# A cross-attention kernel in full-precision halves: softmax ahead of the former batch's probabilities, and a batch's memory in one load

## The chip, the cores and the metric

The kernel runs on 1 core of a Trainium2 chip. The metric is device time in microseconds of one execution. All inputs are in HBM, and the output is written there. Host work that only lays out the inputs is not in the time.

## The reference

Per batch (32 of them), x is 112 x 512 and the memory 375 x 256. In float32:

```
memory_proj = memory @ W_mem.T                      # 375 x 512
scores      = x @ memory_proj.T / sqrt(512)         # 112 x 375
attn        = softmax(scores)
context     = attn @ memory_proj                    # 112 x 512
gate        = sigmoid(concat([x, context]) @ W_gate.T + b_gate)
fused       = x + gate * context
out         = fused * rsqrt(mean(fused**2) + 1e-6) * norm_w
```

## The kernel before

**Reassociation.** The projected memory is never formed. q = x W_mem (112 x 256 per batch) meets the raw memory for the scores; `am` = attn times raw memory (112 x 256); the context is am W_mem.T; and the gate's second half is am times `wga`, a product of two weights made once in the opening.

**Halves.** A float32 product is made of three matmuls on rounded operands: high by high, low by high, high by low. Every operand X therefore exists as `X_hi` (ScalarE, `high`, line 537, a copy that rounds) and `X_lo` (the remainder: DVE `low`, line 694, or POOL `low`, line 878). `product` (lines 357 to 359) runs the high stationary operand first (lines 347 and 349) and the low one last (line 354), so that an attend can begin when `pT_hi` is ready and needs `pT_lo` only for its last third (lines 389 to 399).

**Tiling.** A group is 8 batches, 896 rows of x, 7 tiles of 128 rows; there are 4 groups. A step s handles, in each engine's own written order: the scores and softmax of batch s, the attend of batch s-1, the high and low halves of am of batch s-2, the gate and context product of one tile t = `tile_at(s)`, and the end (gate_context, fuse, square, norm) of the tile before. In steps with s % 8 == 2 there is no tile. `q_pieces_at` puts the products for q into steps with s % 8 in 0, 1, 3 (two of them), 6 and 7; `x_unit_at` the splits of xT. Step 30 handles batches 30 and 31, the second one late (`softmaxes_at`).

**Softmax of batch s.** TensorE's scores go to one PSUM bank. DVE: `maximum` (reduce, line 706, then line 708, which multiplies by -1/sqrt(512)). ScalarE: `exponentials` (line 566, scale 1/sqrt(512), bias the shift, row sum into `total`). DVE: `turn_p` (line 714) transposes 32 x 32 blocks into `blocks_p`; SP moves them in 4 DMAs of 48 KB to `pT_raw` (`move_p`, line 262), which completes the transpose; ScalarE and DVE make `pT_hi`, `pT_lo` (lines 572 and 722). `am` goes the same way: copied out of PSUM by ScalarE (line 579), turned by DVE (line 728), moved by SP in 4 DMAs (line 269), then halved.

**Orders around the change.** In step s, ScalarE: pT_high(s-1), exponentials(s), amT_high(s-2), square, split_memT(s+1), attended(s-1), split_mem(s), q_high, split_xT, tanh (lines 658 to 684). In step 30 split_memT(31) stands before the exponentials. DVE: gate_context, pT_low(s-1), maximum(s), fuse, turn_p(s), shares, amT_low(s-2), turn_am(s-1), norm, q_low, add_bias (lines 836 to 863). POOL: the inverse root for the tile before, memT_lo(s+1), mem_lo(s), xT_lo (lines 911 to 922); in step 30 memT_lo(31) first. TensorE: score(s), gate_x, attend(s-1), q pieces, gate_am, context (lines 512 to 529).

**SP's queue** is one order by hand (lines 281 to 336). In step s: move_p(s), move_am(s-1), load_memT(s+3), load_mem(s+1), an xT unit, and the x rows and the output of a tile. `memT_raw` and `mem_raw` have two slots each; `blocks_p` and `pT_raw` have one, so move_p(n) waits for pT_lo(n-1).

Of the kernel before, what the change touches and what calls it, by code (L numbers as in the profile page):

```python
# [12 lines left out]
P = 128  # L13
# [13 lines left out]
MEMT, MEM = EC * KEVEN, KC * E  # L27
UNITS = [(0, 256), (256, 320), (576, 320)]
# [74 lines left out]
def build_gated_cross_attention(nc, x_d, xT_d, memT_d, mem_d, first_d, wmT_d, wgT_d, b_d, nw_d, out_d):  # L103
    ctx = ExitStack()
    with ctx:
# [10 lines left out]
        first_raw = sb("first_raw", [P, DC // 2 * (E + UNITS[0][1])])  # L116
# [11 lines left out]
        memT_raw = sb("memT_raw", [P, 2, MEMT])  # L128
        mem_raw = sb("mem_raw", [P, 2, MEM])
# [3 lines left out]
        blocks_p = sb("blocks_p", [P, KPAD])  # L133
        pT_raw = sb("pT_raw", [P, KPAD])
        pT_hi, pT_lo = (sb(f"pT_{s}", [P, 2, KC, P], F32R) for s in ("hi", "lo"))
# [6 lines left out]
        top = sb("top", [ROWS, 2])  # L142
# [9 lines left out]
        zeros = blocks_p[:, 0:D // 2].bitcast(BF16)  # L152
# [6 lines left out]
        memT_raws = memT_raw[:].rearrange("p s (c n) -> p s c n", c=EC)  # L159
        mem_raws = mem_raw[:].rearrange("p s (c n) -> p s c n", c=KC)  # L160
        firsts = [first_raw[:], work[:, 4:6].rearrange("p s d -> p (s d)")]
        wm_halves = [a[:, 0:DC // 2 * E].rearrange("p (i e) -> p i e", e=E) for a in firsts]
        x0_halves = [a[:, DC // 2 * E:].rearrange("p (i n) -> p i n", i=DC // 2) for a in firsts]
        wmT_raw = first_raw[:].rearrange("p (c d) -> p c d", c=EC)
# [7 lines left out]
        turned_p = blocks_p[:].rearrange("p (j c r) -> p c j r", j=Q, r=R)  # L172
        pT_flat = pT_raw[:].rearrange("p (q n) -> p q n", q=Q)
        pT_rows = pT_raw[:].rearrange("p (q c r) -> p c q r", q=Q, r=R)
        blocks_p_rows = [blocks_p[R * q:R * (q + 1)].rearrange("p (j n) -> p j n", j=Q) for q in range(Q)]
# [4 lines left out]
        amT_rows = amT_raw[:].rearrange("p (q c r) -> p c q r", q=Q, r=R)  # L180

# [33 lines left out]
        memT_loaded = [sem(f"memT_loaded{i}") for i in range(2)]  # L215
        mem_loaded = [sem(f"mem_loaded{i}") for i in range(2)]
# [6 lines left out]
        scores_done, top_ready, shift_ready = sem("scores_done"), sem("top_ready"), sem("shift_ready")  # L223
        probs_ready, share_ready = sem("probs_ready"), sem("share_ready")
        blocks_p_ready, p_turned = sem("blocks_p_ready"), sem("p_turned")
# [13 lines left out]
        def _(sp):  # L239
# [7 lines left out]
            def load_memT(n):  # L247
                if n >= 2:
                    sp.wait_ge(memT_lo_ready, n - 1)
                sp.dma_start(memT_raw[:, n % 2], memT_d[n]).then_inc(memT_loaded[n % 2], 16)  # L250
# [732 lines left out]
```

## Time and profile before

| | us |
|---|---|
| three plain runs | 334.11, 334.95, 336.81 |
| their median | 334.95 |
| the profiled execution | 332.4 |
| its span | 330.2 |
| TensorE matmul busy | 285.8 (87%) |
| TensorE weight loads | 243.6 (74%) |
| DVE busy | 216.5 (66%) |
| ScalarE busy | 171.7 (52%) |
| POOL busy | 169.7 (51%) |
| DMA, mean share of 16 engines, hardware queue | 60.6% |

The span runs from the first to the last instruction of the profiled execution; its own time is 2.2 us longer. Engines are PE (TensorE matmul), PEld (its weight loads, which overlap the matmuls), DVE, ACT (ScalarE), POOL (GpSimd) and SP, whose queue issues every DMA here (SPq). All rows of instructions with the same form that follow each other are merged into one, with a count. PEclk is the granted TensorE clock as a share of 2.4 GHz.

### The profile page before, as it was taken

The page shows a single profiled execution, that of the slowest core. Times are in us where ns is not written, and L with a number is a line of the kernel's source. Part 1 is how long each engine was busy: PE and PEld are TensorE (multiplying, and loading weights), DVE is VectorE, ACT ScalarE, POOL GpSimd, SP SyncE. Part 2 cuts the span into 40 slices and gives each one's busy share as a digit, 9 for nine tenths or more (in the row PEclk, how much of TensorE's full clock was granted, in tenths as well). Part 3 has the DMA queues.
Part 4 walks back from the last instruction along what each step waited for, and adds up shares of the span by engine and source line. Part 5 has one row for each costly group of instructions (what it writes and reads, how often), then busy time and mean ns, then how long its engine had stood idle before and what let it go on. Part 6 is the DMA issues. An engine that isn't in the chain of part 4 may idle for free.

```text
span 330.2 us, 4795 instructions
## 1 busy us (share of the span) xinstructions
PE 285.8 (87%) x1479; PEld 243.6 (74%) x1479; DVE 216.5 (66%) x388; ACT 171.7 (52%) x363; POOL 169.7 (51%) x135
## 2 busy tenths in 40 slices
PE   8999699899995499999997499999998499996392
PEld 4979488778884498788886498788887398884362
DVE  4995556677676536877577626777777736786344
ACT  5865354457544537456555546546555445553412
POOL 1244248555655544665658544665758543653302
PEclk9999979999999599999999599999999699999787
DMA  7959953757766293866846383766837464652411
GB/s 285 423 152 240 284 185 85 240 187 248 212 186 191 53 276 101 263 201 177 281 136 199 110 267 111 233 207 188 277 92 232 138 199 113 201 147 52 155 48 65
DMA packets 57048, 61.40 MB, mean 186 GB/s; under 512 B 39104, under 2 KB 39360, under 8 KB 56768
## 3 DMA queue, kind: packets, MB, share of 16 engines
q1 hardware_dynamic: 57024, 61.10, 60.6%
q8 instruction: 12, 0.20, 0.2%
q14 instruction: 12, 0.10, 0.1%
HBM read 43.25 MB, written 7.34 MB: 153 GB/s over the span
## 4 chain that ended last, share of the span: by engine, by line
PE 30%; DVE 20%; SPq 13%; DMA 13%; ACT 10%; issue 7%; POOL 5%; DVEq 0%; POOLq 0%
SPq L262 7%; DMA pT_raw<-blocks_p 6%; DVE pT_lo L694 6%; DMA mem_raw<-in_mem 6%; PE gate_ps L347 5%; PE gate_ps L349 4%; PE gate_ps L354 4%; SPq L269 4%; POOL memT_lo L878 3%; DVE work L743 3%; ACT work L593 2%; DVE top L706 2%; DVE work L737 2%; PE score_ps L347 2%; ACT probs L566 2%
## 5 line engine op out<-in xcount | busy, mean ns | idle before, releaser
L878 POOL TENSOR_TENSOR mem_lo<-mem_raw,mem_hi 128x768 fp32r<-128x768 f32 x32 | 68.1, 2129 | 23.4 <-ACT mem_hi L537 23.4
L878 POOL TENSOR_TENSOR memT_lo<-memT_raw,memT_hi 128x752 fp32r<-128x752 f32 x31 | 56.6, 1825 | 30.0 <-ACT memT_hi L537 30.0
L896 POOL TENSOR_TENSOR guarded<-meansq,eps 128x1 f32<-128x1 f32 x27 | 5.1, 190 | 98.7 <-ACT work L588 98.7
L566 ACT ACTIVATE probs<-score_ps,shift 112x375 f32<-112x375 f32 x32 | 18.3, 573 | 56.8 <-DVE shift L708 56.8
L728 DVE STREAM_TRANSPOSE blocks_am<-am 128x256 f32<-128x256 f32 x32 | 14.3, 446 | 42.0 <-ACT am L579 38.8
L694 DVE TENSOR_TENSOR pT_lo<-pT_raw,pT_hi 128x384 fp32r<-128x384 f32 x32 | 33.0, 1031 | 11.6 <-ACT pT_hi L537 11.6
L758 DVE SCALAR_TENSOR_TENSOR work<-work,rstd,norm_w 128x512 f32<-128x512 f32 (+1 forms) x29 | 39.8, 1375 | 1.1 <-POOL rstd L931 1.0
L593 ACT ACTIVATE work<-work 128x512 f32<-128x512 f32 (+1 forms) x29 | 17.8, 616 | 36.3 <-DVE work L737 36.3
L743 DVE SCALAR_TENSOR_TENSOR work<-work,ctx_ps 128x512 f32<-128x512 f32 (+1 forms) x28 | 19.0, 679 | 23.9 <-ACT work L593 22.0
L537 ACT ACTIVATE mem_hi<-mem_raw 128x768 fp32r<-128x768 f32 x32 | 26.9, 840 | 13.7 <-DMA mem_raw<-in_mem 13.7
L347 PE MATMUL gate_ps<-wgx_hi,xT_hi 128*128 128x512 f32 x108 | 32.0, 422 | 0.1
L347 PE MATMUL score_ps<-memT_hi,qT_hi 128*112 128x376 f32 x64 | 18.2, 368 | 15.3 <-POOL memT_lo L878 14.8
L349 PE MATMUL gate_ps<-wgx_lo,xT_hi 128*128 128x512 f32 x108 | 29.8, 399 | 0.0
L354 PE MATMUL gate_ps<-wgx_hi,xT_lo 128*128 128x512 f32 x108 | 28.9, 389 | 0.0
L537 ACT ACTIVATE memT_hi<-memT_raw 128x752 fp32r<-128x752 f32 x32 | 26.2, 820 | 0.0
L347 PEld LDWEIGHTS score_ps<-memT_hi,qT_hi 128*112 128x112 f32 x64 | 11.1, 189 | 20.2 <-issue 17.3
L347 PE MATMUL am_bank<-mem_hi,pT_hi 128*112 128x256 f32 x96 | 17.4, 290 | 9.9 <-POOL mem_lo L878 6.3
L347 PEld LDWEIGHTS am_bank<-mem_hi,pT_hi 128*112 128x112 f32 x96 | 14.6, 178 | 14.6 <-issue 7.1
L537 ACT ACTIVATE pT_hi<-pT_raw 128x384 fp32r<-128x384 f32 x32 | 16.4, 514 | 16.5 <-DMA pT_raw<-blocks_p 16.5
L878 POOL TENSOR_TENSOR xT_lo<-xT_raw,xT_hi 128x1280 fp32r<-128x1280 f32 (+1 forms) x9 | 24.8, 2761 | 0.0
L349 PEld LDWEIGHTS gate_ps<-wgx_lo,xT_hi 128*128 128x128 f32 x108 | 20.9, 194 | 4.9
L347 PEld LDWEIGHTS gate_ps<-wgx_hi,xT_hi 128*128 128x128 f32 x108 | 21.8, 209 | 3.6 <-DVE work L737 0.8
(125 smaller groups left out, 665.0 us busy)
## 6 DMA issues: line engine op xcount, KB each, us to landing
mem_raw<-in_mem SPq DMA_DIRECT2D x32, 384.0 KB, 4.1
memT_raw<-in_memT SPq DMA_DIRECT2D x32, 376.0 KB, 3.5
x_rows<-in_x SPq DMA_DIRECT2D x28, 256.0 KB, 4.5
out<-work SPq DMA_DIRECT2D x27, 256.0 KB, 4.7
pT_raw<-blocks_p SPq DMA_DIRECT2D x128, 48.0 KB, 2.5
xT_raw<-in_xT SPq DMA_DIRECT2D x7, 640.0 KB, 6.3
amT_raw<-blocks_am SPq DMA_DIRECT2D x128, 32.0 KB, 1.9
xT_raw<-in_xT SPq DMA_DIRECT2D x3, 512.0 KB, 5.8
```

What stands on the lines that cost most here:

```text
L262: sp.dma_start(pT_flat[:, q], blocks_p_rows[q]).then_inc(p_turned, 16)
L347: pe.matmul(out, l_hi, r_hi, start=first and i == 0, stop=False)
L349: pe.matmul(out, l_hi, r_lo, start=False, stop=False)
L354: mm = pe.matmul(out, l_lo, r_hi, start=False, stop=last and i == len(lefts) - 1)
L537: return act.activation(out, in_, ACT.Copy)
L566: act.activation(probs[0:ROWS, 0:KEYS], scores[:, 0:KEYS], ACT.Exp, bias=shift[:, n % 2:n % 2 + 1], scale=D ** -0.5, accum_out=total[:, n ...
L593: act.activation(z[:, t % 2, cols], z[:, t % 2, cols], ACT.Tanh, scale=0.5).then_inc(tanh_ready, 1)
L694: return dve.tensor_tensor(out, in_, high.bitcast(F32), ALU.subtract)
L728: dve.transpose(turned_am, am_blocks).then_inc(blocks_am_ready, 1)
L743: dve.scalar_tensor_tensor(out=u[:, cols], in0=z[:, t % 2, cols], scalar=1.0, in1=bank[:, cols], op0=ALU.add, op1=ALU.mult).then_inc(u_rea ...
L758: dve.scalar_tensor_tensor(out=y[:, t % 2, cols], in0=h[:, t % 2, cols], scalar=rstd[:, t % 2:t % 2 + 1], in1=norm_w[:, cols], op0=ALU.mul ...
L878: return pool.tensor_tensor(out, in_, high.bitcast(F32), ALU.subtract)
```

## The change

- **Order.** In each step ScalarE does the exponentials of batch s before pT_high(s-1); DVE does maximum(s), fuse, turn_p(s) and shares(s) before pT_low(s-1). The opening's order on both engines stays.
- **Two buffers.** `blocks_p` and `pT_raw` get two slots and `p_turned` becomes two semaphores, so move_p(n) waits for pT_lo(n-2) only. `pT_hi` and `pT_lo` lie in `wgc_hi`, and pT_high(0) waits for the products that read it.
- **Scale.** 1/sqrt(512) is applied in q_high and q_low. The exponentials lose their scale; the maximum is one reduce with `negate=True`, and the instruction of line 708 is gone.
- **Memory.** From batch 3 on, memT and mem of a batch come in one DMA of 760 KB into one of three slots (the third is `first_raw`), issued in step s for batch s+2 after move_p(s) and move_am(s-1), and waiting for both low halves of the slot's former batch. In the opening memT(2) is issued earlier relative to move_p(0), and mems(3) and mems(4) stand after move_am(0) and move_am(1). The wmT load goes to `work` and waits for the wgc splits.

```diff
+MEMS = MEMT + MEM
+RAW = 3
...
+        blocks_p = sb("blocks_p", [P, 2, KPAD])
+        pT_raw = sb("pT_raw", [P, 2, KPAD])
...
+        raws = [mems_raw[:, 0], mems_raw[:, 1], first_raw[:]]
...
+            def load_mems(n):
+                sp.wait_ge(memT_lo_ready, n - RAW + 1)
+                sp.wait_ge(mem_lo_ready, n - RAW + 1)
+                sp.dma_start(raws[n % RAW], mems_d[n]).then_inc(mems_loaded[n % RAW], 16)
 
             def move_p(n):
                 sp.wait_ge(blocks_p_ready, n + 1)
-                if n >= 1:
-                    sp.wait_ge(pT_lo_ready, n)
+                if n >= 2:
+                    sp.wait_ge(pT_lo_ready, n - 1)
                 for q in range(Q):
-                    sp.dma_start(pT_flat[:, q], blocks_p_rows[q]).then_inc(p_turned, 16)
+                    sp.dma_start(pT_flat[n % 2][:, q], blocks_p_rows[n % 2][q]).then_inc(p_turned[n % 2], 16)
...
             load_mem(0)
-            load_memT(2)
             load_xT(0, 2)
-            move_p(0)
-            sp.wait_ge(wm_hi_ready, 2)
-            sp.wait_ge(wm_lo_ready, 2)
+            sp.wait_ge(wm_hi_ready, 1)
+            sp.wait_ge(wm_lo_ready, 1)
             sp.wait_ge(x0_hi_ready, 1)
             sp.wait_ge(x0_lo_ready, 1)
-            sp.wait_ge(xT_hi_ready, 1)
-            sp.wait_ge(xT_lo_ready, 1)
+            load_memT(2)
+            move_p(0)
             load_mem(1)
+            sp.wait_ge(wgc_lo_ready, DC)
             sp.dma_start(wmT_raw, wmT_d).then_inc(wmT_loaded, 16)
-            load_memT(3)
             move_p(1)
...
             load_mem(2)
             move_am(0)
-            load_memT(4)
+            load_mems(3)
             move_p(2)
...
             move_am(1)
-            load_memT(5)
-            load_mem(3)
+            load_mems(4)
...
-                if s + 3 < BATCHES:
-                    load_memT(s + 3)
-                if s + 1 < BATCHES:
-                    load_mem(s + 1)
+                if s + 2 < BATCHES:
+                    load_mems(s + 2)
...
-                high(qT_hi[:, half, c:c + w], banks[n % 2][:, 0:w]).then_inc(q_hi_ready, 1)
+                act.activation(qT_hi[:, half, c:c + w], banks[n % 2][:, 0:w], ACT.Copy,
+                               scale=D ** -0.5).then_inc(q_hi_ready, 1)
...
                 act.activation(probs[0:ROWS, 0:KEYS], scores[:, 0:KEYS], ACT.Exp,
-                               bias=shift[:, n % 2:n % 2 + 1], scale=D ** -0.5,
+                               bias=shift[:, n % 2:n % 2 + 1],
                                accum_out=total[:, n % 2:n % 2 + 1]).then_inc(probs_ready, 1)
...
-                if s - 1 < BATCHES:
-                    pT_high(s - 1)
                 if late:
                     split_memT(s + 1)
                 for n in softmaxes_at(s)[:1]:
                     exponentials(n)
+                if s - 1 < BATCHES:
+                    pT_high(s - 1)
...
                 dve.wait_ge(scores_done, n + 1)
-                dve.tensor_reduce(top[:, s], scores[:, 0:KEYS], AX.X, ALU.max).then_inc(top_ready, 1)
-                dve.wait_ge(top_ready, n + 1)
-                dve.tensor_scalar(shift[:, s], top[:, s], -D ** -0.5, None, ALU.mult).then_inc(shift_ready, 1)
+                dve.tensor_reduce(shift[:, s], scores[:, 0:KEYS], AX.X, ALU.max, negate=True).then_inc(shift_ready, 1)
...
-                if s - 1 < BATCHES:
-                    pT_low(s - 1)
                 for n in softmaxes_at(s)[:1]:
                     maximum(n)
                 if before is not None:
                     fuse(before)
                 for n in softmaxes_at(s)[:1]:
                     turn_p(n)
                     shares(n)
+                if s - 1 < BATCHES:
+                    pT_low(s - 1)
```

## Rows read from the trace of the kernel before

**Rows 1.** The page: busy times, and granted clock in 40 slices

```profile
PE 285.8 (87%) x1479; PEld 243.6 (74%) x1479; DVE 216.5 (66%) x388; ACT 171.7 (52%) x363; POOL 169.7 (51%) x135
PEclk9999979999999599999999599999999699999787
```

**Rows 2.** Windows, TensorE alone: window, length, busy, clock, DMA share, GB/s

```profile
113.80:176.00 62.20, 61.19 (x334) 0.99 0.68 204
188.80:251.00 62.20, 61.19 (x333) 0.99 0.67 203
```

**Rows 3.** Timeline at boundaries (steps 10, 18): start, us, engine, line, op [idle before <-releaser]

```profile
111.61 0.94 PE L347 MATMUL score_ps<-memT_hi,qT_hi 128*112 128x376 f32 x2 [4.49 <-POOL memT_lo L878]
...
178.09 2.91 POOL L878 TENSOR_TENSOR xT_lo<-xT_raw,xT_hi 128x1280 fp32r<-128x1280 f32 x1
178.34 0.69 DVE L743 SCALAR_TENSOR_TENSOR work<-work,ctx_ps 128x512 f32<-128x512 f32 x1 [0.70 <-ACT work L593]
178.94 2.48 DVE L694 TENSOR_TENSOR pT_lo<-pT_raw,pT_hi 128x384 fp32r<-128x384 f32 x1
181.34 0.54 DVE L706 TENSOR_REDUCE top<-score_ps 112x1 f32<-112x375 f32 x1
181.48 0.60 PE L354 MATMUL am_bank<-mem_hi,pT_lo 128*112 128x256 f32 x3 [1.75 <-DVE pT_lo L694]
182.97 0.62 ACT L588 ACTIVATE work<-work 128x512 f32<-128x512 f32 x1
186.57 0.94 PE L347 MATMUL score_ps<-memT_hi,qT_hi 128*112 128x376 f32 x2 [4.49 <-POOL memT_lo L878]
```

**Rows 4.** Timeline of an ordinary step, 17

```profile
170.29 0.55 DVE L694 TENSOR_TENSOR pT_lo<-pT_raw,pT_hi 128x384 fp32r<-128x384 f32 x1
...
172.00 0.51 PE L347 MATMUL am_bank<-mem_hi,pT_hi 128*112 128x256 f32 x3
...
172.69 0.50 PE L354 MATMUL am_bank<-mem_hi,pT_lo 128*112 128x256 f32 x3
...
173.00 0.82 ACT L537 ACTIVATE memT_hi<-memT_raw 128x752 fp32r<-128x752 f32 x1
...
174.22 0.45 DVE L728 STREAM_TRANSPOSE blocks_am<-am 128x256 f32<-128x256 f32 x1 [1.05 <-ACT am L579]
```

**Rows 5.** Timeline of step 20, from turn_am to the load

```profile
204.78 0.45 DVE L728 STREAM_TRANSPOSE blocks_am<-am 128x256 f32<-128x256 f32 x1 [1.80 <-ACT am L579]
...
207.78 0.59 SPq L250 DMA_DIRECT2D memT_raw<-in_memT  x1
```

**Rows 6.** Landing: mem's issues on the page (last: median us), one in the chain

```profile
mem_raw<-in_mem SPq DMA_DIRECT2D x32, 384.0 KB, 4.1
...
170.22 5.10 DMA mem_raw<-in_mem
```

**Rows 7.** Timeline of the end, steps 30 to 32

```profile
290.62 0.82 ACT L537 ACTIVATE memT_hi<-memT_raw 128x752 fp32r<-128x752 f32 x1
290.69 0.59 SPq L255 DMA_DIRECT2D mem_raw<-in_mem  x1
...
292.18 0.57 ACT L566 ACTIVATE probs<-score_ps,shift 112x375 f32<-112x375 f32 x1 [0.74 <-DVE shift L708]
...
300.70 0.61 PE L347 MATMUL am_bank<-mem_hi,pT_hi 128*112 128x256 f32 x3 [2.53 <-ACT pT_hi L537]
...
304.03 0.59 SPq L255 DMA_DIRECT2D mem_raw<-in_mem  x1
...
310.97 0.95 PE L347 MATMUL am_bank<-mem_hi,pT_hi 128*112 128x256 f32 x3 [6.10 <-POOL mem_lo L878]
```

**Rows 8.** Windows after that: busy of PE, PEld, DVE, ACT, POOL; clock, DMA share

```profile
311.00:316.00 5.00, 5.00 (x17) 4.32 (x18) 2.15 (x5) 1.20 (x3) 0.74 (x2) 0.50 0.03 7
```

**Rows 9.** Timeline of the opening

```profile
29.32 0.82 ACT L537 ACTIVATE memT_hi<-memT_raw 128x752 fp32r<-128x752 f32 x1
...
32.83 0.51 PE L347 MATMUL score_ps<-memT_hi,qT_hi 128*112 128x376 f32 x2
...
41.58 0.71 PE L347 MATMUL gate_ps<-wga_hi,amT_hi 128*128 128x512 f32 x2 [3.34 <-ACT amT_hi L537]
```

More of the change, by code:

```diff
@@ L180, in build_gated_cross_attention @@
         amT_rows = amT_raw[:].rearrange("p (q c r) -> p c q r", q=Q, r=R)
+        pT_hi, pT_lo = (wgc_hi[:].rearrange("p c d -> p (c d)")[:, i * 2 * KPAD:(i + 1) * 2 * KPAD].rearrange(
+            "p (s c n) -> p s c n", s=2, c=KC) for i in range(2))
         def pT_slot(a, n):
@@ L547, in split_memT @@
             def split_memT(n):
-                act.wait_ge(memT_loaded[n % 2], 16 * (n // 2 + 1))
-                high(memT_hi[:, n % 2], memT_raws[:, n % 2]).then_inc(memT_hi_ready, 1)
+                if n < RAW:
+                    act.wait_ge(memT_loaded[n], 16)
+                else:
+                    act.wait_ge(mems_loaded[n % RAW], 16 * (n // RAW + 1))
+                high(memT_hi[:, n % 2], memT_raws[n % RAW]).then_inc(memT_hi_ready, 1)
             def split_mem(n):
-                act.wait_ge(mem_loaded[n % 2], 16 * (n // 2 + 1))
-                high(mem_hi[:, n % 2], mem_raws[:, n % 2]).then_inc(mem_hi_ready, 1)
+                act.wait_ge(mems_loaded[n % RAW], 16 * (n // RAW + 1))
+                high(mem_hi[:, n % 2], mem_raws[n % RAW]).then_inc(mem_hi_ready, 1)
             def q_high(g, unit, half, banks=q_ps):
@@ L721, in pT_low @@
                 dve.wait_ge(pT_hi_ready, n + 1)
-                low(pT_slot(pT_lo, n), pT_rows, pT_slot(pT_hi, n)).then_inc(pT_lo_ready, 1)
+                low(pT_slot(pT_lo, n), pT_rows[n % 2], pT_slot(pT_hi, n)).then_inc(pT_lo_ready, 1)
             def turn_am(n):
@@ L800, in _ @@
             dve.wait_ge(memT_hi_ready, 1)
-            low(memT_lo[:, 0], memT_raws[:, 0], memT_hi[:, 0]).then_inc(memT_lo_ready, 1)
+            low(memT_lo[:, 0], memT_raws[0], memT_hi[:, 0]).then_inc(memT_lo_ready, 1)
             q_low(0, 1, 0)
@@ L886, in split_memT @@
                 pool.wait_ge(memT_hi_ready, n + 1)
-                low(memT_lo[:, n % 2], memT_raws[:, n % 2], memT_hi[:, n % 2]).then_inc(memT_lo_ready, 1)
+                low(memT_lo[:, n % 2], memT_raws[n % RAW], memT_hi[:, n % 2]).then_inc(memT_lo_ready, 1)
             def split_mem(n):
                 pool.wait_ge(mem_hi_ready, n + 1)
-                low(mem_lo[:, n % 2], mem_raws[:, n % 2], mem_hi[:, n % 2]).then_inc(mem_lo_ready, 1)
+                low(mem_lo[:, n % 2], mem_raws[n % RAW], mem_hi[:, n % 2]).then_inc(mem_lo_ready, 1)
             def inverse_rms(t):
@@ L967 @@
         "xT": xT,
-        "memT": chunked(memT).reshape(BATCHES, P, MEMT),
-        "mem": chunked(turned_rows(padded(memory, 1, KPAD))).reshape(BATCHES, P, MEM),
+        "mems": np.concatenate([chunked(memT).reshape(BATCHES, P, MEMT),
+                                chunked(turned_rows(padded(memory, 1, KPAD))).reshape(BATCHES, P, MEM)], axis=2),
         "first": np.concatenate([chunked(w_memT.T).reshape(P, 2, DC // 2 * E),
```

67 lines of the change are left out of this document (32 added, 35 removed).

## The prediction, made before the changed kernel ran

> **What bounds the kernel now.** I read the page first. TensorE is busy 87% of the span, no other engine over 66%, and the granted clock falls five times [rows 1]. So the question is where TensorE isn't busy. Cut by window, it is busy 61.19 us of 62.20 in the long stretch between two group boundaries, and as much in the next one [rows 2]. A microsecond saved elsewhere is worth nothing there, and a microsecond that TensorE has to wait is lost whole. Its idle time lies in three places: the opening (3.34 us ahead of the gate's product at 41.58 [rows 9]); the group boundary, three times (1.75 and 4.49 us [rows 3]); and the last two batches (2.53 and 6.10 us [rows 7]). After the last of these the granted clock is 0.50 of full, 1.2 GHz, for 5.00 us in which TensorE is busy throughout [rows 8]: that costs another 2.5.
>
> The boundary (steps 10, 18, 26) is a step with no tile, so TensorE has only 2 us of its own work and the softmax chain is exposed. In step 18, `pT_lo` of batch 17 takes 2.48 us where the same operation takes 0.55 in an ordinary step, since POOL's `xT_lo` runs from 178.09 to 181.00; the maximum starts only at 181.34, then exponentials, fuse, square (182.97), POOL's inverse root and its `memT_lo`, and the scores of batch 19 start at 186.57 [rows 3].
>
> The profiled execution took 332.4 us for a span of 330.2; the three plain runs have a median of 334.95, 2.55 above it. I work out a difference against the profiled one and put it on the median. A measurement can tell about 1% here (3.3 us).
>
> **Maximum and exponentials first, at the boundary.** gate_context (one input in PSUM) took 0.69 us in spite of POOL's split [rows 3], so the maximum, which reads PSUM, should not be held either: it starts when gate_context ends, at 179.1, 2.2 us earlier; without L708 the exponentials start 0.55 later, at 179.7. Next on DVE is the fuse. It reads two SBUF operands, as `pT_lo` does, so it takes over the collision: POOL is done at 181.0, and pT_lo ended 0.4 after that; I put the fuse's end at 181.5. The square then starts at 181.55 instead of 182.97, and square to scores stays 3.60: 185.15. That is -1.4 a boundary, three times -4.2. Bounds: -3 (a fuse that isn't held) and +0.5 (`pT_hi` of batch 17, now done before the exponentials, comes behind them, at 180.5, and its attend starts at 181.05, some 2.3 later than now; if that lets the clock fall one step longer, the gain is gone). I take the middle, nearest to the pT_lo row.
> The Trainium skill (SBUF — State Buffer, section SBUF: two separate sides) says that a DVE operation with two SBUF inputs and a GpSimd operation take a shared port in turn, each for its whole instruction. By that rule too the fuse ends at about 181.0 plus its own 0.7, 181.7, and the boundary gives 1.2 instead of 1.4. The trace agrees with it (2.48 against 0.55).
>
> **The same order in the covered stretches.** Step 17 [rows 4]: pT_lo ends at 170.84, and the attend wants pT_hi at 172.00 and pT_lo at 172.69. After: maximum at 170.3, where pT_lo stood (TensorE's scores are there by then), 0.54 long, exponentials at 171.0, done with their accumulator read at 171.75, pT_hi 171.8 to 172.3: 0.3 late. Turned probabilities from 171.7, 0.58; reciprocal 0.12; pT_lo 0.55: ends at 173.0, wanted (0.3 later by now) at 173.0. So 0.3 us in such a step. Against it: the exponentials come 0.75 sooner (0.55 of pT_lo, 0.2 for L708 and its wait), pT_high (0.51) now stands between them and the copy of am, so that copy and what follows it on DVE come 0.25 sooner, and part of the loss is made good. In the step behind the other xT split the fuse is held as at the boundary and pT_lo comes behind it: up to 1.2 late, once a group. Together, between -0.5 and +3 a group.
>
> **The memory's loads.** This is where I see the cost. Before, memT of a batch is issued 3 steps ahead, mem one step. After, both come in one transfer issued in step s for batch s+2, behind the moves of that step, and the first half is wanted in step s+1, ahead of the copy of am on ScalarE. That closes a ring which was not there: turn_am, four SP issues (2.5), load, landing, memT_hi, am, turn_am. From rows: turn_am at 204.78 to the load's issue at 207.78 is 3.00 [rows 5]; mem, issued some 0.6 behind memT (its issue lasts 0.59), lands 4.1 after its issue (median [rows 6]), so both are there 4.7 after the first issue, and the joined transfer, which moves the same bytes with one issue less, is put at the same 4.7; from the start of memT_hi (173.00) to that of turn_am (174.22) it is 1.22 [rows 4], with the handover ahead 1.3. Sum 9.0 to 9.1 us a step. Before, eight steps took 75.0 (the scores at 111.61 to those at 186.57 [rows 3]). One of them has two pieces of q and takes TensorE 11.1 of its own work; 11.1 + 7 x 9.1 = 74.8. So the ring sits just at the mean of the steps: it costs nothing where TensorE needs more, and steps of 7.6 to 8.5 (no q piece) can no longer run ahead. Bounds: 0, and, with the landing of 5.10 that the chain shows at 170.22, 5.7 with the issue ahead [rows 6], 7 x 1.0 = +7 a group. I take +1.2 a group for ring and late halves together, three groups: +3.6.
> The Trainium skill speaks both ways here (DMA: Bandwidth & Descriptors, section Rules for kernel authors): larger transfers reach more bandwidth, and a load should be issued early and waited for late. In this trace the second counts: memT is issued up to three steps ahead now, one after. By the first, the joined load would land before 4.7; no row here shows it.
>
> **The opening.** memT of batch 3 was loaded early and split at 29.32; after, it comes with mem behind move_am(0), where memT(4) is issued now, at about 29.6; by 4.7 it lands at 34.3. ScalarE holds attended(1), amT_high(0), mem_high(2) behind it, TensorE's scores of batch 3 start at 37.1 instead of 32.83 [rows 9]: 1.8 for the two splits' handover and POOL's half are in it. The stall of 3.34 at 41.58 takes most of that back: it waits for amT of batch 1, whose move is held by the queue of x loads. Net +1 at 45, and with the ring binding in the next five steps TensorE is about 2.5 late at step 10. The boundary's idle time takes that up except for 0.5. Value +0.5, bounds 0 and +3. The alias of pT_hi on wgc_hi waits for matmuls that end before the probabilities land: nothing. q's scale in q_high and q_low is in instructions that are there already: nothing, and nothing plausible on either side.
>
> **The end.** Before, mem(31) is issued at 304.03, since SP stood at move_p(31), and the two splits and attend(31) at 310.97 follow [rows 7]. After, it comes with memT(31), issued in step 29 near 291.2 (the load of that step was issued at 290.69), and 4.4 later, with little else in the queue, it is there: 295.6. But in step 30 ScalarE splits memT(31) first (290.62) and then does the exponentials (292.18 [rows 7]): they now start at 296.5, 4.3 late. Counting on by durations of the same operations: pT_hi(29) 297.3, attend(29) 297.8, where TensorE went from step 29 to it without a pause before; attend 1.03, scores 1.2, gate 1.4, bias 0.7, tanh 0.65, pT_hi 0.5: attend(30) at 303.4 (was 300.70); am's move lands 304.9, amT_hi, square, am, mem_hi to 307.4, mem_lo 1.85: attend(31) at 309.4. So the 6.10 and 2.53 of idle mostly turn into idle before attend(29), gain -1.5. What goes with it is the slow clock: TensorE waits little before attend(31), so 5.00 us at 0.50 become 2.5 at 1.00: -2.5. Together -4.0; bounds -11 (the load isn't late) and 0 (fallen clock in steps 30 and 31 instead).
>
> **Sum.** -4.2 + 3.6 + 0.5 - 4.0 = -4.1: 328.3 profiled, and 330.9 on the median, say 331.0.
>
> **The rivals.**
> 1. Slower by the ring, 340. Landings as at 170.22 in half of the steps: 3.4 a group in place of 1.2, +6.6, one more late load in the opening (+1), one at the end (+1): -4.1 + 8.6 = +4.5, and with rounding 340. It decides from a mean landing of about 5.2 (ring 9.6, +3.5 a group). For it: such a landing stands in the trace; x, xT and output transfers share the queue. Against: the median is 4.1, and one issue goes away. Chance 0.22.
> 2. The loads are hidden, 320. Ring 0, exponentials of batch 30 on time, and both waits of the end gone: -4.2 + 0.5 - 8.6 - 2.5 = -14.8. For it: three slots, and the slot is free in time. Against: the load stands behind two moves on SP. Chance 0.14.
> 3. Late probabilities, 336. pT_hi and pT_lo cost 0.3 in some 20 steps without being made good (+6), less the 1 counted: +1. For it: TensorE is 98% busy in the stretches. Against: DVE's round shortens. Chance 0.14.
> 4. The new order does nothing at the boundary (fuse as late as pT_lo was, clock slow longer), 335: -4.1 + 4.2. Chance 0.12.
> The forecast, 327.5 to 334.5: 0.38.
>
> **The numbers.** Faster by over 1% (under 331.6): rival 2 and somewhat more than half of the forecast's band and its neighbours, 0.41. Within 1%: the rest of the band, rivals 3 and 4, 0.36. Slower: rival 1, 0.23. The range runs from 323 to 341; the likeliest case has 327.5 to 334.5.
>
> **What would show it.** Right: in steps 10, 18, 26 the maximum starts within 0.2 us of gate_context's end and the fuse takes over 1.5 us; scores of the next step 1 to 2 us sooner; memT_hi shows waits for the joined load in many steps; TensorE idle about 4 us before attend(29), under 1.5 before attend(31), no slow clock behind it; turn_am to turn_am near 9.1 in steps without q. Wrong: memT_hi never waits for a load (rival 2), or landings over 5.2 and steps of 9.6 and more (rival 1), or attends waiting for pT in most steps (rival 3).

## The result, and the profile after

The changed kernel takes 344.50 us (median of four runs, 341.96 to 344.70) against 335.11 for the kernel before on the same chip: a ratio of 1.0257, 95% interval 1.0194 to 1.0321. The forecast was 331.0 with a range to 341, so the sign was wrong and the time lies above the range. The profiled execution took 344.57 us, its span is 342.8. The spans of the two profiled executions differ by 12.6 us; the times by 9.4 on the medians. Two runs of the experiments below lie far outside the others (408.21 us in two_loads, 1005.77 us in opening) and are left out, so medians and ratios are of the undisturbed runs.

The page of the kernel after, busy times and granted clock in 40 slices, to be read against [rows 1]:

```profile
PE 295.7 (86%) x1479; PEld 246.7 (72%) x1479; DVE 210.1 (61%) x356; ACT 173.7 (51%) x363; POOL 173.3 (51%) x135
PEclk9999699999999599999999589999999689998997
```

No engine took over: DVE, ScalarE and POOL have no larger share than before. The same page, groups of instructions (busy us, mean ns, then the idle time ahead of them and what ended most of it) and DMA issues (KB each, median us to landing):

```profile
L736 DVE STREAM_TRANSPOSE blocks_am<-am 128x256 f32<-128x256 f32 x32 | 14.2, 445 | 70.5 <-ACT am L588 70.5
...
L540 ACT ACTIVATE memT_hi<-mems_raw 128x752 fp32r<-128x752 f32 x22 | 18.3, 831 | 34.6 <-DMA mems_raw<-in_mems 34.5
...
mems_raw<-in_mems SPq DMA_DIRECT2D x20, 760.0 KB, 5.1
...
first_raw<-in_mems SPq DMA_DIRECT2D x9, 760.0 KB, 4.8
```

The second line is the new thing. ScalarE's `memT_hi` stood idle for the joined load, 34.5 us in all for the two slots of `mems_raw` (and 9.0 more for the third, `first_raw`); DVE's turn_am, which stands behind it through the copy of am, waited 70.5 us.

The timeline of an ordinary step without a stall in TensorE's own row shows the ring whole, that is, the chain that leads from one turn_am over the load back to the next turn_am:

```profile
221.79 0.45 DVE L736 STREAM_TRANSPOSE blocks_am<-am 128x256 f32<-128x256 f32 x1 [1.46 <-ACT am L588]
222.26 2.48 SPq L277 DMA_DIRECT2D amT_raw<-blocks_am  x4
...
224.84 0.54 SPq L263 DMA_DIRECT2D first_raw<-in_mems  x1
...
230.05 0.84 ACT L540 ACTIVATE memT_hi<-first_raw 128x752 fp32r<-128x752 f32 x1 [1.75 <-DMA first_raw<-in_mems]
...
230.96 1.82 POOL L886 TENSOR_TENSOR memT_lo<-first_raw,memT_hi 128x752 fp32r<-128x752 f32 x1 [1.76 <-ACT memT_hi L540]
...
231.28 0.45 DVE L736 STREAM_TRANSPOSE blocks_am<-am 128x256 f32<-128x256 f32 x1 [2.86 <-ACT am L588]
...
233.04 0.57 PE L350 MATMUL score_ps<-memT_hi,qT_hi 128*112 128x376 f32 x2
```

From turn_am to the load's issue 3.05 us, from the issue to memT_hi 5.21, from memT_hi to the next turn_am 1.23: 9.49. The next turn_am starts at 240.78, again 9.50 later. TensorE is tied in by POOL: memT_lo ends at 232.78, the scores start at 233.04. The starts of three other turn_am give the mean:

```profile
134.54 0.45 DVE L736 STREAM_TRANSPOSE blocks_am<-am 128x256 f32<-128x256 f32 x1 [1.65 <-ACT am L588]
...
201.75 0.45 DVE L736 STREAM_TRANSPOSE blocks_am<-am 128x256 f32<-128x256 f32 x1 [3.37 <-ACT am L588]
...
212.89 0.45 DVE L736 STREAM_TRANSPOSE blocks_am<-am 128x256 f32<-128x256 f32 x1 [1.65 <-ACT am L588]
```

The first two lie seven steps apart, 67.2 us: 9.6 a step. The eighth is the step with two pieces of q and takes 11.14, as it did before (11.12). Together they are 78.35, the length of a group.

What that does to TensorE stands in windows of TensorE alone (window, length, busy, clock, DMA share, GB/s). Each runs from the scores behind one boundary to the scores at the next (batches 11 to 18), the first before the change, the second after, and holds the same 346 records of matmuls:

```profile
111.61:177.59 65.98, 64.97 (x346) 0.98 0.66 196
```

```profile
115.29:185.14 69.85, 67.94 (x346) 0.96 0.64 185
```

The same work takes 3.9 us longer, and in the next group (batches 19 to 26) again 3.9 (69.98 for 66.05). Only 0.9 of it shows as idle; busy rose from 65.0 to 67.9, and the busy share alone would have hidden the loss. Part of that busy time is a slower clock. The first 6 us behind the second boundary, before and after:

```profile
186.57:192.57 6.00, 6.00 (x25) 0.73 0.62 170
```

```profile
193.46:199.46 6.00, 6.00 (x16) 0.53 0.65 183
```

TensorE is busy throughout in both, but after the change it gets half the clock (1.2 GHz) for nearly all of it. Behind the other two boundaries it is 0.56 for 0.75 and 0.51 for 0.71. That is 1.2 us a group (an estimate: 6 us times the difference). The rest of the rise wasn't traced row by row.

The boundary, step 18, timeline, to be read against [rows 3]:

```profile
186.22 2.90 POOL L886 TENSOR_TENSOR xT_lo<-xT_raw,xT_hi 128x1280 fp32r<-128x1280 f32 x1
186.24 0.69 DVE L751 SCALAR_TENSOR_TENSOR work<-work,ctx_ps 128x512 f32<-128x512 f32 x1 [0.70 <-ACT work L602]
...
186.84 0.54 DVE L716 TENSOR_REDUCE shift<-score_ps 112x1 f32<-112x375 f32 x1
187.30 2.36 DVE L758 SCALAR_TENSOR_TENSOR work<-work,x_rows 128x512 f32<-128x512 f32 x1
...
188.55 0.71 PE L350 MATMUL am_bank<-mem_hi,wgc_hi 128*112 128x256 f32 x3 [2.22 <-ACT wgc_hi L540]
...
189.70 0.63 ACT L597 ACTIVATE work<-work 128x512 f32<-128x512 f32 x1 [0.90 <-DVE work L758]
...
193.46 0.94 PE L350 MATMUL score_ps<-memT_hi,qT_hi 128*112 128x376 f32 x2 [1.77 <-POOL memT_lo L886]
```

The maximum starts as gate_context ends (186.84 and 186.93, the two overlap slightly), the fuse takes over the collision with POOL and ends 0.54 us after POOL's xT_lo, and the attend waits for pT_hi (written to `wgc_hi` now). All of that is as forecast. From gate_context to the next scores it is 7.22 us, against 8.23 in [rows 3].

The opening, timeline, against [rows 9]:

```profile
29.76 0.53 SPq L263 DMA_DIRECT2D mems_raw<-in_mems  x1
...
35.01 0.83 ACT L540 ACTIVATE memT_hi<-mems_raw 128x752 fp32r<-128x752 f32 x1 [6.10 <-DMA mems_raw<-in_mems]
...
37.98 0.94 PE L350 MATMUL score_ps<-memT_hi,qT_hi 128*112 128x376 f32 x2 [5.09 <-ACT qT_hi L566]
```

And the end, timeline of steps 30 and 31, against [rows 7]; the window below it (busy of PE, PEld, DVE, ACT, POOL; clock, DMA share, GB/s) against [rows 8]:

```profile
303.82 0.54 SPq L263 DMA_DIRECT2D mems_raw<-in_mems  x1
...
308.78 0.83 ACT L540 ACTIVATE memT_hi<-mems_raw 128x752 fp32r<-128x752 f32 x1 [4.73 <-DMA mems_raw<-in_mems]
309.51 0.56 ACT L573 ACTIVATE probs<-score_ps,shift 112x375 f32<-112x375 f32 x1
...
310.62 0.60 PE L350 MATMUL am_bank<-mem_hi,wgc_hi 128*112 128x256 f32 x3 [4.12 <-ACT wgc_hi L540]
```

```profile
312.00:317.00 5.00, 5.00 (x19) 4.50 (x20) 2.76 (x7) 1.87 (x4) 0.71 (x2) 0.68 0.28 59
```

The load of the last batch (issued at 303.82, memT_hi at 308.78) holds the exponentials of batch 30 and through them attend(29), and the clock still falls behind that wait (0.68 over these 5 us).

A ledger by where the scores of batches 3, 11, 19 and 27 start, read from the timelines of the profiled executions (us; the last column is from batch 27's scores to the span's end). The lower rows are experiments, told below:

| kernel | to batch 3 | 3 to 11 | 11 to 19 | 19 to 27 | rest |
|---|---|---|---|---|---|
| before | 32.8 | 78.8 | 75.0 | 74.9 | 68.8 |
| after | 38.0 | 77.3 | 78.2 | 78.3 | 71.1 |
| order_alone | 33.3 | 75.6 | 73.2 | 72.5 | 66.9 |
| loads_first | 38.1 | 71.0 | 72.6 | 72.3 | 63.7 |
| two_loads | 36.5 | 70.7 | 73.3 | 74.0 | 65.1 |
| loads_mid | 38.0 | 71.7 | 74.9 | 74.5 | 64.3 |
| boundary | 33.5 | 70.7 | 71.3 | 70.8 | 62.3 |

Against before, the changed kernel loses 5.2 in the opening, wins 1.5 of it back by batch 11, loses 3.2 and 3.4 in the two middle groups and 2.3 at the end: 12.6.

### The profile page after: what moved, and what is told of

The parts are those of the page before. It is cut to its first block and busy times, and to the rows that moved or that the text cites. A ratio compares the mean times of both kernels' runs of the same rounds, so it can differ in the third digit from the quotient of the medians.

```text
span 342.8 us, 4761 instructions
## 1 busy us (share of the span) xinstructions
PE 295.7 (86%) x1479; PEld 246.7 (72%) x1479; DVE 210.1 (61%) x356; ACT 173.7 (51%) x363; POOL 173.3 (51%) x135
## 5 line engine op out<-in xcount | busy, mean ns | idle before, releaser
L886 POOL TENSOR_TENSOR memT_lo<-mems_raw,memT_hi 128x752 fp32r<-128x752 f32 x21 | 38.1, 1815 | 58.8 <-ACT memT_hi L540 58.8
L736 DVE STREAM_TRANSPOSE blocks_am<-am 128x256 f32<-128x256 f32 x32 | 14.2, 445 | 70.5 <-ACT am L588 70.5
L886 POOL TENSOR_TENSOR mem_lo<-mems_raw,mem_hi 128x768 fp32r<-128x768 f32 x22 | 48.1, 2188 | 10.6 <-ACT mem_hi L540 10.5
L904 POOL TENSOR_TENSOR guarded<-meansq,eps 128x1 f32<-128x1 f32 x27 | 5.5, 203 | 78.3 <-ACT work L597 78.2
L540 ACT ACTIVATE memT_hi<-mems_raw 128x752 fp32r<-128x752 f32 x22 | 18.3, 831 | 34.6 <-DMA mems_raw<-in_mems 34.5
L758 DVE SCALAR_TENSOR_TENSOR work<-work,x_rows 128x512 f32<-128x512 f32 (+1 forms) x29 | 34.4, 1189 | 0.3
L350 PE MATMUL gate_ps<-wgx_hi,xT_hi 128*128 128x512 f32 x108 | 33.2, 433 | 0.1
L352 PE MATMUL gate_ps<-wgx_lo,xT_hi 128*128 128x512 f32 x108 | 31.8, 419 | 0.0
L350 PE MATMUL am_bank<-mem_hi,wgc_hi 128*112 128x256 f32 x96 | 18.3, 300 | 12.8 <-ACT wgc_hi L540 10.8
L350 PEld LDWEIGHTS am_bank<-mem_hi,wgc_hi 128*112 128x112 f32 x96 | 14.0, 179 | 19.6 <-ACT wgc_hi L540 18.0
L357 PE MATMUL am_bank<-mem_hi,wgc_hi 128*112 128x256 f32 x96 | 19.1, 311 | 9.5 <-DVE wgc_hi L703 9.4
L352 PEld LDWEIGHTS gate_ps<-wgx_lo,xT_hi 128*128 128x128 f32 x108 | 22.3, 206 | 5.4
L886 POOL TENSOR_TENSOR memT_lo<-first_raw,memT_hi 128x752 fp32r<-128x752 f32 x10 | 18.7, 1871 | 12.5 <-ACT memT_hi L540 12.5
```

What stands on the lines that cost most here:

```text
L350: pe.matmul(out, l_hi, r_hi, start=first and i == 0, stop=False)
L352: pe.matmul(out, l_hi, r_lo, start=False, stop=False)
L357: mm = pe.matmul(out, l_lo, r_hi, start=False, stop=last and i == len(lefts) - 1)
L540: return act.activation(out, in_, ACT.Copy)
L736: dve.transpose(turned_am, am_blocks).then_inc(blocks_am_ready, 1)
L758: dve.scalar_tensor_tensor(out=h[:, t % 2, cols], in0=u[:, cols], scalar=0.5, in1=x_rows[:, t % X_SLOTS, cols], op0=ALU.mult, op1=ALU.add) ...
```

## The experiments

The kernel before was run beside each on the same chip; ratios are to it.

**loads_first.** The changed kernel with its joined load issued at the head of SP's step, ahead of both moves. The same edit of place serves as the base of later experiments.

```diff
             for s in range(OPENING, STEPS):
+                if s + 2 < BATCHES:
+                    load_mems(s + 2)
                 for n in softmaxes_at(s)[:1]:
                     move_p(n)
...
-                if s + 2 < BATCHES:
-                    load_mems(s + 2)
```

> The changed kernel, with the joined load of batch s+2 issued at the head of SP's step s, before the moves of p and am, not behind them. Theory A (a ring: turn_am, move_am, joined load, memT_hi, copy of am, 9.5 us a step): the ring is cut, memT_hi stops waiting, a group of eight steps falls from 78.2 us to 75 or less, the exponentials of batch 30 come on time; 344.5 falls to 331 to 336. The opening keeps its 3 us. Theory B (the later halves of the probabilities starve TensorE): loads don't matter, 342 to 346.

318.95 us, ratio 0.9495 (0.9449 to 0.9540). Two lines moved on one queue are worth 25.6 us, and the kernel is then 5% faster than the one before. That is 12 us below the range that the ring theory had given: it had reckoned with groups of 75 us or less, and they take 71.0 to 72.6. One step of its timeline beside the ring above:

```profile
156.89 0.38 SPq L263 DMA_DIRECT2D mems_raw<-in_mems  x1
...
159.87 2.50 SPq L270 DMA_DIRECT2D pT_raw<-blocks_p  x4
160.01 0.82 ACT L540 ACTIVATE memT_hi<-first_raw 128x752 fp32r<-128x752 f32 x1
...
162.47 2.50 SPq L277 DMA_DIRECT2D amT_raw<-blocks_am  x4
```

The load leaves 3 us ahead of the first move of its step and 8 us ahead of the place behind both moves (162.47 + 2.50) where the changed kernel has it. memT_hi doesn't wait for one here; over the whole execution it waits twice, both in the opening (5.66 and 3.30 us). The landing is longer than after the change, 6.0 and 6.2 us on the median, as the same page's DMA issues say, and costs nothing:

```profile
mems_raw<-in_mems SPq DMA_DIRECT2D x20, 760.0 KB, 6.0
...
first_raw<-in_mems SPq DMA_DIRECT2D x9, 760.0 KB, 6.2
```

Its window from the scores of batch 11 to those of batch 18 (TensorE alone, columns as above) is back at 65.8 us, for 345 records:

```profile
109.12:174.94 65.82, 65.35 (x345) 0.97 0.65 196
```

The Trainium skill (DMA: Bandwidth & Descriptors, section Rules for kernel authors) says to issue a transfer early and wait for its semaphore late. The runs agree: the longer landing that left early cost 25 us less than the shorter one that left late.

**old_order.** The changed kernel with ScalarE's and DVE's former order in each step.

```diff
+                if s - 1 < BATCHES:
+                    pT_high(s - 1)
                 if late:
                     split_memT(s + 1)
                 for n in softmaxes_at(s)[:1]:
                     exponentials(n)
-                if s - 1 < BATCHES:
-                    pT_high(s - 1)
...
+                if s - 1 < BATCHES:
+                    pT_low(s - 1)
                 for n in softmaxes_at(s)[:1]:
                     maximum(n)
...
                     shares(n)
-                if s - 1 < BATCHES:
-                    pT_low(s - 1)
```

> The changed kernel with ScalarE's and DVE's old order in the steps (pT_high before the exponentials, pT_low before the maximum); loads, two buffers and scale stay changed. Theory A: the ring doesn't pass through these, so the groups stay at 77 to 79 us and the boundary's stall comes back on top: 344 to 349. Theory B: back to 334 to 338.

352.11 us, ratio 1.0496 (1.0432 to 1.0560), 3 us above the range of the first theory: the order is worth 7.6 us even with the ring in place. It isn't the order that made the kernel slower.

**order_alone.** The kernel before with the new order and the two buffers for probabilities (`pT_hi` and `pT_lo` in `wgc_hi`, as after, to make room), and with its own loads and scales.

> The kernel before with only the new order and the two buffers for turned probabilities (pT halves in wgc_hi); separate loads in their old places, L708 and the scales as before. Theory A: the order is worth 1 to 2 us at each of three boundaries and some at the end: 327 to 333. Theory B: slower than 335.1 by 3 to 8, 338 to 343.

323.99 us, ratio 0.9629 (0.9563 to 0.9696), 12.2 us less than the kernel before beside it and 3 us below the range of the first theory. The ledger shows 1.7 to 3.2 less in each group and 1.9 less at the end. At the boundary the scores of batch 18 start at 175.09 and those of batch 19 at 182.07, 6.98 apart, where the kernel before has 177.59 and 186.57, 8.98: 2.0 less.

**two_loads.** The changed kernel with each joined load cut in two at the same place of SP's queue, memT's part first, so that memT_hi waits for 376 KB only.

```diff
-                sp.dma_start(raws[n % RAW], mems_d[n]).then_inc(mems_loaded[n % RAW], 16)
+                sp.dma_start(raws[n % RAW][:, 0:MEMT], mems_d[n, :, 0:MEMT]).then_inc(memT_loaded[n % RAW], 16)
+                sp.dma_start(raws[n % RAW][:, MEMT:MEMS], mems_d[n, :, MEMT:MEMS]).then_inc(mems_loaded[n % RAW], 16)
```

> The changed kernel with the joined load cut in two DMAs, memT then mem, issued one behind the other at the same place in SP's queue; ScalarE's split of memT waits for the first alone. Theory A: memT lands 3.3 to 3.5 us after its issue where the joined load took 5.1, the ring falls from 9.5 to 7.9 and no longer binds in most steps: groups 75 to 76, total 334 to 338, opening 1 us better. Theory B, and a theory that only the place in the queue matters and not the size: 342 to 346.

323.56 us, ratio 0.9614 (0.9551 to 0.9677), 10 us below what the ring theory had given. The page gives the landings of both parts:

```profile
mems_raw<-in_mems SPq DMA_DIRECT2D x22, 384.0 KB, 3.9
mems_raw<-in_mems SPq DMA_DIRECT2D x22, 376.0 KB, 3.5
```

memT is there 1.6 us sooner than in one transfer (3.5 against 5.1), so the ring should fall from 9.5 to about 7.9 (an estimate from these landings), and that alone gives 20.9 us. The place in the queue stayed, only the length of one link changed, so the place isn't all that matters. A shorter landing would also help a load that was merely late, without a ring, and this run can't tell the two apart. That it is a ring stands in the timeline above, where each link starts as the one before it ends and the last leads back to the first.

**am_first.** The changed kernel with `attended(s-1)` ahead of `split_memT(s+1)` on ScalarE, to take the copy of am out of the ring.

> The changed kernel with one swap on ScalarE in each step: the copy of am of batch s-1 before the split of memT of batch s+1. Loads stay where the change put them, and land 5.1 us after their issue. Theory A (it is a ring through the copy of am): the ring is cut at another place, groups fall from 78.2 to 73 to 76 us, total 322 to 330, though memT_hi still waits for its load. Theory C (the late load costs by itself, wherever ScalarE stands, since memT_lo and the scores come late): little changes, 340 to 345.

342.08 us, ratio 1.0184 (1.0108 to 1.0260). The ring theory had given 322 to 330, its rival (the late load costs by itself) 340 to 345, and the time lies with the rival. Its cause is another, though. The wait for the load did fall; what is left stands in the opening and at the end:

```profile
L540 ACT ACTIVATE memT_hi<-mems_raw 128x752 fp32r<-128x752 f32 x22 | 18.1, 824 | 12.3 <-DMA mems_raw<-in_mems 12.3
```

But memT_hi now stands behind the attend, and the timeline shows another chain:

```profile
219.57 0.62 PE L357 MATMUL am_bank<-mem_hi,wgc_hi 128*112 128x256 f32 x3 [0.47 <-DVE wgc_hi L703]
220.28 0.47 ACT L588 ACTIVATE am<-am_bank,share 112x256 f32<-112x256 f32 x1 [2.01 <-issue]
220.65 0.82 ACT L540 ACTIVATE memT_hi<-mems_raw 128x752 fp32r<-128x752 f32 x1
...
221.55 1.97 POOL L886 TENSOR_TENSOR memT_lo<-mems_raw,memT_hi 128x752 fp32r<-128x752 f32 x1 [1.29 <-ACT memT_hi L540]
...
223.78 0.57 PE L350 MATMUL score_ps<-memT_hi,qT_hi 128*112 128x376 f32 x2 [0.80 <-POOL memT_lo L886]
```

From the attend's end (220.19) the scores come 3.6 us later, where TensorE has only gate and context to do. The groups take as long as after the change (76.2, 78.3 and 78.4). In ordinary steps no load is waited for here, so its lateness can't be what they cost. One chain was cut and another made, and this run tells nothing of the size of the first.

**loads_mid.** The changed kernel with the load between move_p(s) and move_am(s-1): behind the probabilities, no longer behind am.

> The changed kernel with one edit on SP: the joined load for batch s+2 is issued after move_p(s) but ahead of move_am(s-1), so no load waits for turn_am(s-1). Theory (ring through turn_am): the ring of 9.5 us is cut, ScalarE's memT_hi no longer waits for a load in ordinary steps, groups fall from 78.2 to under 74 us, total 318 to 324. Rival (a load behind the probabilities' move is late too, because it is issued after turn_p): the load leaves 3 us sooner but still takes 5 to 6 us beside the moves, groups stay over 76, total 330 or more.

325.91 us, ratio 0.9697 (0.9645 to 0.9750): most of the gain (18.6 of 25.6), but 1.9 us above what the ring theory had given. The link from turn_am to the load is cut, and memT_hi waits for a load three times only, in the opening and at the end (11.0 us in all). The load also leaves some 3 us sooner, so a load that was merely late would have gained as well. The timeline shows what stays:

```profile
137.56 0.54 SPq L263 DMA_DIRECT2D mems_raw<-in_mems  x1
...
138.19 2.48 SPq L277 DMA_DIRECT2D amT_raw<-blocks_am  x4
...
144.88 0.42 ACT L540 ACTIVATE amT_hi<-amT_raw 128x256 fp32r<-128x256 f32 x1 [2.79 <-DMA amT_raw<-blocks_am]
...
145.82 0.82 ACT L540 ACTIVATE memT_hi<-mems_raw 128x752 fp32r<-128x752 f32 x1
```

The load for batch 15 leaves at 137.56, and memT_hi of batch 15 starts only 8.26 later. But it doesn't wait for that load: ahead of it on ScalarE stands amT_hi, which waits 2.79 for am, and the move of am is now the transfer that is issued directly behind 760 KB. Its median landing is 3.1 us here, against 1.9 in loads_first and after the change, and ScalarE waits for it 18 times, 14.2 us in all (3 times and 3.4 us in loads_first). So what is left isn't a late load, which the rival had expected, but a late move of am. That the load in front of it causes this is argued from the order of the queue and the landings; no run took it apart.

**one_buffer, scale_back.** loads_first with the waits of a single buffer for the probabilities; and loads_first with the scale in the exponentials and L708's instruction again.

> The kernel of loads_first with the waits of a single buffer of turned probabilities: move_p(n) waits for pT_lo(n-1), turn_p(n) for the move of n-1. If the second buffer is what makes the new order work (pT_lo now ends 1.2 us behind turn_p, and SP's queue stands there): 325 to 332, moves of p a good microsecond later in each step. If it only matters for batches 30 and 31: 320 to 322.

> The kernel of loads_first with the scale in the exponentials again and the maximum in two instructions. If the 0.2 us of each maximum lies on the path of every step: up to 5 us slower, 322 to 324. If it lies on the path only at the three boundaries and in the last steps: 319.5 to 320.5.

322.21 us, ratio 0.9575 (0.9496 to 0.9653), and 322.19, ratio 0.9583 (0.9510 to 0.9656): each 3.2 to 3.3 above loads_first on the medians, which were taken on another chip. one_buffer is nearer to its second case (320 to 322), scale_back lies in its first (322 to 324). The intervals overlap with that of loads_first, so each is a likely 3 us and not a proven one.

**opening.** loads_first with the opening's loads earlier: load_mems(3) after load_mem(1), load_mems(4) after move_am(0).

> The kernel of loads_first (319.0) with two loads of the opening moved forward: the joined load of batch 3 ahead of wmT and move_p(1), that of batch 4 ahead of move_p(2). Theory A2 (the opening's 4.6 us of TensorE's wait for the scores of batch 3 is that load alone): 314 to 316.5. Theory B2 (the opening's wait passes to the move of am of batch 1 behind the loads of x, 3.7 us as in order_alone): 318 to 320.

318.99 us, ratio 0.9489 (0.9390 to 0.9588): by the medians no gain, as the second theory had it. In the profiled execution the span is 314.7 against 317.7. The scores of batch 3 start at 33.15 instead of 38.09, and the gate's product then waits 3.45 us for amT at 41.78, as before the change [rows 9]. What the 5 us of the opening are worth in the end (0 to 3) stays open.

**act_back.** loads_first with ScalarE's former order alone (pT_high ahead of the exponentials); DVE keeps the new one.

> loads_first with one edit on ScalarE: pT_high(s-1) again ahead of the exponentials of batch s, as before the change; DVE keeps maximum, fuse, turn_p ahead of pT_low. It asks which half of the new order gives its 12 us. Theory A (the gain comes from exponentials that no longer stand behind a wait for the moved probabilities): the gain is lost, 328 to 332. Theory B (it comes from DVE, where the maximum no longer stands behind pT_low): at most 3 us are lost, 319 to 322.

317.13 us, ratio 0.9465 (0.9419 to 0.9511): nothing lost, 2 us below the range of the second theory. So here the order's gain doesn't need ScalarE's half; it is DVE's, where the maximum no longer stands behind pT_lo.

**boundary.** opening with another order in steps 10, 18 and 26 alone:

```diff
+                border = tile_at(s) is None and s < BATCHES - 2
-                if late:
+                if late or border:
                     split_memT(s + 1)
+                if border:
+                    pT_high(s - 1)
                 for n in softmaxes_at(s)[:1]:
                     exponentials(n)
...
```

DVE makes pT_lo between maximum and fuse in these steps, and POOL memT_lo ahead of the inverse root.

> The kernel called opening with another order in steps 10, 18 and 26 alone, where TensorE still idles 1.75 us ahead of the attend and 2.35 us ahead of the next scores: ScalarE makes memT_hi of the next batch and pT_hi of the former one while it would wait for the maximum, DVE makes pT_lo ahead of the fuse, and POOL makes memT_lo ahead of the inverse root. Theory (the two gaps are queueing behind work that can go later): 2.5 to 3.5 us less at each boundary, 8 to 10 in all, 309 to 312. Rival (what is moved behind, the exponentials and the fuse, is late next, and the gap comes back one batch on): 316 to 320.

310.42 us, ratio 0.9261 (0.9227 to 0.9295), within the theory's range and the fastest kernel of this case. The timeline of step 18:

```profile
171.83 0.51 ACT L540 ACTIVATE wgc_hi<-pT_raw 128x384 fp32r<-128x384 f32 x1
...
172.39 0.61 PE L350 MATMUL am_bank<-mem_hi,wgc_hi 128*112 128x256 f32 x3 [0.22 <-ACT wgc_hi L540]
...
173.21 2.09 POOL L892 TENSOR_TENSOR memT_lo<-mems_raw,memT_hi 128x752 fp32r<-128x752 f32 x1
...
173.58 2.26 DVE L761 SCALAR_TENSOR_TENSOR work<-work,x_rows 128x512 f32<-128x512 f32 x1
...
175.55 0.57 PE L350 MATMUL score_ps<-memT_hi,qT_hi 128*112 128x376 f32 x2 [1.23 <-POOL memT_lo L892]
```

The attend waits 0.22 us instead of 2.22 after the change, and the scores come 4.6 us after those of batch 18 (170.97), where loads_first has 6.8. The fuse is held behind POOL again (2.26), but nothing of TensorE waits for it now.

**best.** boundary with pT_high ahead of the exponentials in every step; the name was given before it ran.

> The kernel called boundary with one more edit on ScalarE: pT_high(s-1) stands ahead of the exponentials in every step (as before the change), while DVE keeps the new order. Theory (the ScalarE half of the new order is worth nothing, or costs up to 2 us, as act_back against loads_first says): 308 to 310.5. Rival (the 1.8 us between act_back and loads_first came from the boundary steps, which boundary has already mended; with the DVE order new, pT_lo waits for nothing more): 310.5 to 312, no gain.

312.48 us, ratio 0.9332 (0.9288 to 0.9377): 2.1 slower than boundary, and slower than either expectation gave. What act_back had hinted at doesn't carry over: with the boundaries mended, the exponentials' early place looks worth about 2 us. The two ran on different chips and their intervals just touch, so this is likely and not proven, and why they differ was not traced.

## Why the prediction was wrong

**The step that failed** is in "The memory's loads": the landing of 4.7 us, with it the ring of 9.0 to 9.1 us a step, and with that the price of +1.2 a group. The other two links were right: 3.05 against 3.00 from turn_am to the issue, and 1.23 against 1.22 (1.3 with the handover) from memT_hi to turn_am. The joined transfer landed after 5.1 us on the median, 5.21 with the handover in the step shown, and from turn_am to turn_am the seven steps between boundaries take 9.6 on the mean. At 0.5 more than the forecast's 9.1 they are 3.5 us a group, and the groups took 78.2 and 78.3 where it made 74.8. The stretch that the price was meant for came out 3.9 us longer instead of 1.2. The 4.7 was built from a single transfer's landing plus the issue of the one ahead of it. That mixes where a 384 KB transfer ends with how long 760 KB take; the row that showed 5.10 was set aside as an end of the range.

The terms of the sum against what the two profiled executions show (us; the scores of a batch mark the ends):

| stretch | forecast | measured |
|---|---|---|
| to the scores of batch 10 (the opening, and 1.2 for the first group) | +1.7 | +5.2 |
| the three boundaries | -4.2 | -2.7 |
| batches 11 to 18 and 19 to 26 | +2.4 | +7.8 |
| from batch 27 to the end | -4.0 | +2.3 |
| sum | -4.1 | +12.6 |

The forecast's 0.5 for the opening was what would be left of 2.5 behind the first boundary; the measured first row ends ahead of it.

The slower clock behind each boundary (0.51 to 0.56 for 0.71 to 0.75 over 6 us) is in the third row and was in no term. It is 1.2 of each 3.9 at most, since some of it is made good: the scores of batch 12 come 1.1 later for their step than before, and by batch 14 0.5 of that is back. Other kernels have it at times: two_loads, with its shorter ring, behind the second boundary (0.53), and that group takes 74.0 us where the one before it (0.68) takes 73.3. So the clock is worth about 1 us of a group there, not the whole 3.9 (an estimate from these two groups; no run isolates it).

**The comparison was off as well.** The ring was held against the mean step of the kernel before (75.0 by eight), and "costs nothing where TensorE needs more" was read from that. But the new order shortens the groups to 72.5 and 73.2 where no ring binds (order_alone), and the scale and the early load carry this to 72.3 and 72.6 (loads_first). A ring at the old mean eats every gain made elsewhere. That is what happened: against loads_first it takes 6.3, 5.5, 6.0 and 7.4 us in the four stretches of the ledger behind batch 3, 25 in all. Rival 1 had the mechanism and nearly the size: a landing of 5.2 and a ring of 9.6, +3.5 a group, against 5.1, 9.6 and +3.9. Its 340 was still 4.5 short, for the opening and the end.

**The opening** was put at +0.5. Up to the scores of batch 3 the forecast held (37.1 for 37.98, and a landing at 34.3 where memT_hi started at 35.01). Then it failed. The delay was to shrink to 1 by about 45 us, to be 2.5 at step 10 and to be taken up by the boundary except for 0.5. The scores of batch 4 start 3.0 late (48.70 for 45.67), those of batch 10 5.2 late, and those of batch 11 still 3.7. In loads_first they start 2.5 earlier than before in spite of the same late batch 3, so the delay can be made good, but not while a ring sets the pace of the steps between.

**The end** was put at -4.0 and came out at +2.3. The load of batch 31 was to leave at 291.2. It left at 303.82, 12.6 later: the scores of batch 27 were 10.3 late and those of batch 29, in whose step it is issued, 11.5. So the exponentials of batch 30, forecast at 296.5, came at 309.51. The stall ahead of attend(29) that the forecast had named is there (4.12), those before attend(30) and attend(31) shrank to 1.16 and 0.83, but with the ring in the steps before them the last stretch is 7.4 us longer than in loads_first. And the slow clock, which was to vanish, stayed behind the stall, if less of it (0.68 for 0.50 over 5 us). In loads_first, with the same order of ScalarE in step 30, the load isn't late, and the end gives -5.1.

**The boundary** was right in its mechanism and a little high in place: from gate_context to the scores 1.0 less instead of 1.4, because the square to scores took 3.76 for 3.60 (189.70 to 193.46) and because the same late load that held memT_hi pushed POOL's mem_lo and so xT_lo behind it; gate_context and xT_lo start together here (186.24, 186.22), where xT_lo led by 0.25 in [rows 3]. Counted from scores to scores (batch 18 to 19), the changed kernel wins 0.7 of the 8.98, and order_alone, free of the ring, 2.0. The Trainium skill (SBUF — State Buffer, section SBUF: two separate sides) says that a DVE operation with two SBUF inputs waits for a GpSimd operation that holds the shared port. The trace agrees: the fuse took 2.36 us beside xT_lo and has a median of 0.68, and pT_lo, which took 2.48 there before, has a median of 0.53.

**The late halves** were priced at up to 3 us a group. In order_alone the two middle groups are 1.7 and 2.3 shorter, where the one boundary measured gives 2.0, so the price was within 0.3 of nothing. **The scale** was priced at nothing in q, and the missing L708 at a few tenths in a chain that is mostly covered; scale_back says about 3 us over the kernel, likely and not proven.

What stays open: whether the opening's late batch 3 costs anything in a kernel without the ring, how much of the last 2 us between boundary and best is ScalarE's order in ordinary steps; and why the clock stays low for longer behind the boundaries of the changed kernel. The joined load was never put into the kernel before by itself, so what it costs there is known only through old_order.

## What to carry to other kernels

When a change moves a load behind something computed from the step before, write down the ring it closes (what releases the issue, the landing, what it releases) and hold its length against the step time that the rest of the change will leave, not the present mean; a ring equal to the mean cancels every other gain. Put loads whose slot is already free at the head of a step's queue: here a transfer that landed 1 us later but left 8 us sooner cost nothing. Ask also what the load then stands in front of (loads_mid). And when a change bundles several edits, its sum says little of them: here a part worth 12 us by itself (order_alone) and a load whose place cost 25 against a better one (loads_first) stood in the same diff.

## What the runs showed that was not expected

A joined transfer of 760 KB landed after 5.1 us where its first 376 KB alone landed after 3.5 and the rest, issued behind it, after 3.9; a wait for the whole delayed the part that was wanted first by 1.6 us, and on the ring that was worth 20.9 us of 344.5. The landing of that same transfer was longest (6.0 and 6.2) in the kernel where it did no harm. And TensorE's busy time rose by 9.9 us (285.8 to 295.7) for the same 1479 matmuls, part of it at half the clock behind the boundaries, so that a kernel 2.6% slower shows nearly the same busy share, 86% for 87%.
